# 123 products that nobody reads, added to TensorE's stream at 22 places of a gated cross-attention and expert block

## The reference

```python
x = x + tanh(g_xattn) * xattn(layernorm(x), ctx, ctx, mask)   # block A: 16 heads of 16, masked softmax
x = x + tanh(g_ffn) * ffn(layernorm(x))                       # block B
# ffn(y): q, k from rope(y), v from y, causal softmax, 16 heads; out projection
#   x1 = layernorm(y + attn_out) * ln1_w + ln1_b              # u in the kernel
#   gates = softmax(x1 @ gate_w.T + gate_b); the best 2 of 8 experts
#   moe = sum over the chosen of gate * (x1 @ expert_w[e].T + expert_b[e])
#   return layernorm(x1 + moe) * ln2_w + ln2_b
```

## Time and profile before

| | |
|---|---|
| runs | 854.07, 847.18, 850.0 us; median 850.0 |
| the profiled execution | 849.53 us, its span 847.8 |
| granted clock over the span | 0.954 |
| PE busy | 765.9 us (90%), 9348 matmuls |
| DVE, ACT, POOL busy | 665.2 (78%), 564.3 (67%), 470.3 us (55%) |
| DMA | 20.71 MB, q1 at 8.3% of 16 engines |
| chain that ended last | PE 59%, ACT 20%, DVE 15%, issue 4%, POOL 1% |

### The profile page before, as it was taken

How to read it: one execution, slowest core, us unless ns; L and a number is a source line. 1 busy time by engine, 2 the same in 40 slices (tenths; PEclk the granted TensorE clock), 3 DMA queues, 4 the chain that set the end, 5 groups by cost and what they waited for, 6 DMA issues and landing times.

```text
span 847.8 us, 23991 instructions
## 1 busy us (share of the span) xinstructions
PE 765.9 (90%) x9348; PEld 616.1 (73%) x9348; DVE 665.2 (78%) x1908; ACT 564.3 (67%) x1268; POOL 470.3 (55%) x854
## 2 busy tenths in 40 slices
PE   5558789999999999999999999999999999988885
PEld 3446677878778777778778778778787787766663
DVE  4473659797897979797988979797978978786765
ACT  4576767777677777678676777677776777764310
POOL 7242445666564656666564646566665646455343
PEclk8588989999999999999999999999999999999877
DMA  7410000010010101010010101010100000000000
GB/s 200 121 55 15 15 15 16 8 35 10 2 37 8 36 8 36 8 36 9 15 29 2 37 8 36 8 36 9 33 11 2 8 8 9 9 8 7 7 13 13
DMA packets 33568, 20.71 MB, mean 24 GB/s; under 512 B 11672, under 2 KB 33456, under 8 KB 33456
## 3 DMA queue, kind: packets, MB, share of 16 engines
q1 hardware_dynamic: 33456, 19.19, 8.3%
HBM read 14.99 MB, written 4.19 MB: 23 GB/s over the span
## 4 chain that ended last, share of the span: by engine, by line
PE 59%; ACT 20%; DVE 15%; issue 4%; POOL 1%; DMA 0%; SPq 0%; DVEq 0%; POOLq 0%
PE bank L395 29%; PE bank L510 8%; PE bank L529 7%; ACT bank L718 6%; DVE neg_max_A L965 6%; ACT bank L727 5%; DVE moe L1074 3%; ACT probs_B L768 3%; PE bank L579 3%; PE bank L550 3%; PE bank L568 2%; ACT probs_A L768 2%; PE bank L404 2%; PE bank L540 1%; DVE neg_max_B L965 1%
## 5 line engine op out<-in xcount | busy, mean ns | idle before, releaser
L1286 POOL TENSOR_SCALAR_AFFINE_SELECT probs_B<-probs_B 128x512 f32<-128x512 f32 x128 | 77.2, 641 | 186.5 <-ACT probs_B L768 186.5
L1074 DVE SCALAR_TENSOR_TENSOR moe<-bank,gates,moe 128x256 f32<-128x256 f32 x256 | 123.1, 481 | 51.7 <-PE bank L395 37.3
L727 ACT ACTIVATE bank<-mask_add 128x512 f32<-128x512 bf16 x128 | 76.6, 602 | 51.1 <-DVE neg_max_A L965 51.1
L395 PE MATMUL bank<-w_expertsa,u_t_a 128*128 128x512 f32 x256 | 107.5, 420 | 0.5 <-ACT o_raw L776 0.5
L395 PE MATMUL bank<-w_expertsa,u_t_b 128*128 128x512 f32 x256 | 103.2, 403 | 0.0
L395 PE MATMUL bank<-w_expertsb,u_t_a 128*128 128x512 f32 x256 | 103.1, 403 | 0.0
L965 DVE TENSOR_REDUCE neg_max_A<-bank 128x4 f32<-128x512 f32 x128 | 79.4, 682 | 12.1 <-PE bank L510 11.7
L965 DVE TENSOR_REDUCE neg_max_B<-bank 128x4 f32<-128x512 f32 x128 | 79.3, 681 | 5.7 <-PE bank L510 5.7
L718 ACT ACTIVATE bank<-mask_add 128x512 f32<-128x512 bf16 x128 | 69.8, 627 | 0.0
L718 ACT ACTIVATE bank<-causal_add 128x512 f32<-128x512 bf16 x128 | 69.7, 623 | 0.0
L768 ACT ACTIVATE probs_A<-bank 128x512 f32<-128x512 f32 x128 | 66.1, 603 | 4.7 <-PE bank L550 2.3
(11 more groups left out here) (222 smaller groups left out, 2417.0 us busy)
## 6 DMA issues: line engine op xcount, KB each, us to landing
x_in<-in_x SPq DMA_DIRECT2D x32, 128.0 KB, 2.3
ctx_t<-in_ctxT SPq DMA_DIRECT2D x32, 128.0 KB, 2.2
out<-y_out SPq DMA_DIRECT2D x32, 128.0 KB, 1.7
w_stage<-in_expertsT SPq DMA_DIRECT2D x8, 256.0 KB, 3.9
mask_u<-in_masks SPq DMA_DIRECT2D x32, 32.0 KB, 2.1
w_stage<-in_in_projT SPq DMA_DIRECT2D x3, 256.0 KB, 4.7
w_stage<-in_WkT SPq DMA_DIRECT2D x1, 256.0 KB, 2.9
w_stage<-in_WvT SPq DMA_DIRECT2D x1, 256.0 KB, 3.4
```

Of the source, the lines that this page charges most:

```text
L395: done = pe.matmul(out_ap, l, r, start=n == 0, stop=n == len(terms) - 1)
L727: act.activation(score_banks[g][:].rearrange("p (h k) -> p h k", k=P), mask_add[t % MASK_SLOTS][:, 1:2, :].to_broadcast([P, GROUP, P]), AC ...
L1074: dve.scalar_tensor_tensor(out=moe[(e + 1) % 2][:], in0=bank[:, (e % 2) * EMBED:(e % 2 + 1) * EMBED], scalar=gates[:, e:e + 1], in1=moe[e ...
L1286: pool.affine_select(out=part, in_=part, compare_op=ALU.is_ge, fill=0.0, base=0, pattern=[[0, GROUP], [1, P]], channel_multiplier=-1).then ...
```

## The change

A helper `keep_busy(use, t, count)` waits as `take_work(use, t)` does and then multiplies the bf16 identity with itself `count` times, 512 columns each, into the bank that the real use of that name fills next. The real use starts its own accumulation afresh, so nothing of these products is ever read. 22 calls are put into PE's program, in rounds 0 to 2 and 16 to 18, with counts from 2 to 13 that add up to 123. The other engines' programs stay as they are.

```diff
+            def keep_busy(use, t, count):
+
+                bank = take_work(use, t)
+                for _ in range(count):
+                    pe.matmul(bank[:], ident_bf[:], ident_bf[:].unsqueeze(1).to_broadcast([P, GROUP, P]), start=True, stop=True)
...
+                if r == 1:
+                    keep_busy("A_out", 0, 3)
                 project_o("A", 2 * r - 2)
+                if r == 0:
+                    keep_busy("x_t", 0, 5)
                 x_t(2 * r)
...
+                if r == 1:
+                    keep_busy("A_max_t", 1, 11)
+                if r == 2:
+                    keep_busy("A_max_t", 3, 11)
                 scores_t("A", 2 * r - 1)
...
+                if r == 1:
+                    keep_busy("A_values", 1, 4)
                 attend("A", 2 * r - 1)
...
+                if r == 0:
+                    keep_busy("A_k", 0, 2)
                 project_k_a(r)
+                if r == 18:
+                    keep_busy("gate", 31, 7)
                 gate(2 * r - 5)
                 normalise("A", 2 * r - 1)
                 project_v_a(2 * r)
+                if r == 17:
+                    keep_busy("B_max_t", 31, 6)
                 scores_t("B", 2 * r - 3)
...
+                if r == 1:
+                    keep_busy("A_out", 1, 4)
                 project_o("A", 2 * r - 1)
+                if r == 0:
+                    keep_busy("A_q", 0, 3)
                 project_q_a(r)
...
+                if r == 0:
+                    keep_busy("A_max_t", 0, 3)
+                if r == 1:
+                    keep_busy("A_max_t", 2, 3)
+                if r == 2:
+                    keep_busy("A_max_t", 4, 4)
                 scores("A", 2 * r)
                 attend("B", 2 * r - 3)
+                if r == 18:
+                    keep_busy("bias", 31, 2)
                 expert_bias_sum(2 * r - 5)
                 expert_pair(1, 2 * r - 5)
+                if r == 0:
+                    keep_busy("A_max_t", 0, 11)
+                if r == 1:
+                    keep_busy("A_max_t", 2, 13)
+                if r == 2:
+                    keep_busy("A_max_t", 4, 8)
                 scores_t("A", 2 * r)
...
+                if r == 17:
+                    keep_busy("B_normalise", 31, 4)
                 normalise("B", 2 * r - 3)
                 u_transposed(2 * r - 4)
+                if r == 1:
+                    keep_busy("y_t", 0, 4)
                 y_transposed(2 * r - 2)
                 scores("B", 2 * r - 2)
+                if r == 0:
+                    keep_busy("A_values", 0, 4)
                 attend("A", 2 * r)
...
+                if r == 16:
+                    keep_busy("B_max_t", 30, 8)
                 scores_t("B", 2 * r - 2)
                 transpose_max("B", 2 * r - 2)
+                if r == 0:
+                    keep_busy("A_o_t", 0, 3)
                 o_transposed("A", 2 * r)
```

## The result

| | before | after the change |
|---|---|---|
| median of 10 runs each | 850.0 us | 844.1 us (839.0 to 846.3) |
| ratio to before | | 0.9923, 95% interval 0.9897 to 0.9949 |
| span of the profiled execution | 847.8 us | 842.4 us |
| granted clock over the span | 0.954 | 0.986 |
| PE busy | 765.9 us | 776.1 us |

The change makes the kernel 0.8% faster, 6 us, where 845 us was forecast. It lies inside the 1% for which the forecast gave 0.64.

What follows compares the result with a forecast made beforehand. PE bounds the middle at clock 1.00; in the ramp a chain of waits between PE, ACT and DVE does, slowed by low clock. Ramp -2.8 and tail -1.8 make -4.6 us: 845 us, range from one below 838 to 852.

Steps and rivals of the forecast that it cites:

- the 1% for which the forecast gave 0.64: Whole kernel: changes under 1% (8.5 us) cannot be told from none; chance of landing within that 0.64.
- The time: Whole kernel: forecast 845 us against a median of 850.0, chance 0.57.
- The eight groups behind a wait: Eight of 22 groups run after PE's idle time, delaying real work: 2.8 us in the ramp, 3.6 in the tail.
- The high price: One added bf16 product of 512 columns on PE at the higher clock level: 0.233 us, from fp32 products.
- The cover: Products inside PE's waits cost nothing: ahead of L529, 11 take 2.6 us in 3.2, 13 take 3.0 in 4.26.
- The gain of the ramp: Up to about 125 us: -8.5 gained, +2.8 for exposed groups, +2.9 for likely clock falls, sum -2.8 us.
- The start: Ahead of 16 us PE is tied to ACT, so only 0.3 us of the first products' gain arrives.
- The tail: From 781 us on: -2.3 + 2.0 - 1.7 - 1.8 + 0.9 + 0.6 + 0.5, sum -1.8 us.
- clock high everywhere: Rival: the clock stays high at all these places in ramp and tail, -11.7, so 838 us; chance 0.24.
- Absorbed ramp: Rival: ACT's and DVE's weight splitting and loads hold the first tiles, only the tail counts: 848 us; chance 0.13.
- Overshoot: Rival: products do not hold the clock, cost 0.42 us each and overrun the waits: +22 us, 872 us; chance 0.06.
- Clock low at every unfilled place: Clock falls at every unfilled wait, products behind at 0.42 us: +3.4, 853 us; upper end of forecast, no own chance.

Runs made afterwards that it cites:

- experiment 1: The change without the eight groups that stand behind a wait, leaving 14 groups (90 products), against the kernel before: 838.1 us, ratio 0.9870.
- experiment 2: Only the eight groups behind a wait (33 products), the other 14 left out, against the kernel before: 852.9 us, ratio 1.0031.
- experiment 3: All 22 groups, the eight moved into PE's wait by writing a free bank, 13 more products, against the kernel before: 832.3 us, ratio 0.9801.
- experiment 4: Two runs against the kernel before: only the 17 groups of rounds 0 to 2, 847.1 us (0.9962); only the five of rounds 16 to 18, 847.7 us (0.9975).
- experiment 5: The change with only the six products ahead of tile 31's block B scores moved to a free bank, against the kernel before: 839.8 us, ratio 0.9876.
- experiment 7: The kernel of experiment 3 with its eight long groups cut to three products each: 841.6 us, ratio 0.9898 to the kernel before.

## Why the prediction was right, step by step

- **The time**, 845 us against 844.1: right, and in part by luck. In the profiled execution the ramp gave 1.5 us where 2.8 was forecast and the tail 3.9 where 1.8 was; the two errors have opposite signs. The single executions ran from 839 to 846.
- **The eight groups behind a wait: right in place, too small in price.** All eight stand where the prediction put them, behind PE's idle time. Their cost on the path in the change's trace: 0.95, 1.26 (31.54 to 32.80), 1.56 (51.14 to 52.70), 0.44, 3.03 (795.64 to 798.67), 0.88, 0.5 and 0.33 us, about 9.0 together, where 6.4 was forecast for them at the high level. The first, second, third and fifth ran partly or wholly at the low level, each behind a wait that had not been filled; the forecast had allowed for that at the first, the second and the fifth, in other terms of its sum. That experiments 1, 2 and 3 give them -4.5, +2.6 and -10.4 us is no contradiction: leaving them out loses some clock, having them alone gains some, moving them gets the time back and fills the wait too.
- **The high price** of a product: forecast 0.233 us, from the nearest fp32 row. The 11 at 18.93 take 2.55 with a last record of 0.38: (2.55 - 0.38) / 10 = 0.217. The figure of about 216 ns that the Trainium skill (TensorE: Matmul & The Clock Gate, Back-to-back issue gap) gives by its formula for the gap of a single matmul agrees with the trace, and the row I preferred was the worse neighbour.
- **The cover** by PE's waits: right. The 11s, 8s and the 13 end 0.35 to 1.4 us ahead of the real work.
- **The gain of the ramp**: right in sum by experiment 4 (-2.8 forecast, -3.2 measured, interval -5.3 to -1.2), less in the change's own trace (-1.5). Per tile 1.18 us was forecast; 3.33 became 2.14. The clock fell behind both waits that the prediction named (at 14.0 and 31 us), and a third time behind the 1.44 us at 51.1. I had ruled that out because the same wait brought no fall before; behind the same wait and the same four products it brought none in experiment 5 either, so the program alone does not decide it. A fourth fall, at 116 us behind a wait of 1.87, is in no term of the sum: the scores and `attend` under it take 3.71 us for 2.16 before, most of the 1.7 us between the 3.2 gained up to tile 4 and the 1.5 left at 768.
- **The start**: ACT's copy of xn_t moved from 13.50 to 12.51, more than the 0.3 us that I allowed it. What then held the chain was no engine but a load of the bias row, 3.24 us from its issue at 8.15.
- **The tail**: right in sum by experiment 4 (-1.8 forecast, -2.1 measured), short by half in the change's own trace (-3.9). There one term was far off. At 781 to 787 us 2.7 came back for 2.3 forecast. Ahead of 801 us I forecast +2.0, the clock staying low: the six cost 3.0, but the clock was high again from 799, and 18 projections and expert products took 3.08 for 5.42: net +0.4 in this execution. With the tail's five groups alone (experiment 4) those 18 took 4.38, the clock being low until 805 us: this gain too differs between executions.
- **The rivals**: *clock high everywhere* (838) did not come in the median, but nearly in one of the ten executions of the change: 839.0 us at a mean clock of 0.994, the next 840.7 at 0.991, the other eight 843.6 to 846.3 at 0.984 to 0.987. With the eight moved the clock was nearly as high throughout (0.995), and then the time was 832, since the 6.4 us that this rival still paid were gone too. *Absorbed ramp* (848): excluded for the ramp by experiment 4. *Overshoot* (872): the products do hold the clock, and fit. *Clock low at every unfilled place* (853): it fell behind four of the eight, and twice more, at 116 us behind a wait of 1.87 and at 816 behind one of 0.99.

**Left open.** How far PE must be filled for the clock to stay cannot be read from these runs: a wait of 3.55 us in experiment 7 brought no fall at once, one of 1.44 us in the change did. The executions of one kernel spread by 7 us (839 to 846 for the change), and where the clock falls differs between profiles, even over stretches in which the programs are the same; I did not test what sets that.

## What to carry to other kernels

Products that nobody reads are worth trying where PE waits in a stretch that is bound by latency: here, in waits mostly of 2.1 to 4.3 us, they gave 2% with the right places and 0.8% with eight of 22 in the wrong ones. Look in the instruction order at what the first of them waits for. If it is the same semaphore as the real work's, or a later one, the filler starts when the work could, delays it by its whole length, and the wait stays empty; with a target buffer whose last reader is long done it starts inside the wait. Size the group by the high price and leave it shorter than the wait: filling a fifth instead of four fifths lost 8 us, and twice as many products in the long groups, more than their waits hold, lost 8 to 9 us.

Where the clock falls differs from one execution to the next of the same instructions. Read the cost of a place from a trace, and the gain of a version from the median of many executions.

## What the runs showed of the hardware that was not expected

- fp32 transposes of 128 columns (0.11 us apart) hold the clock at 1.00 as well as bf16 products do.
- The mean granted clock alone does not rank kernels. In the profiled executions it was 0.985 with the groups doubled at 852.2 us, 0.986 with the change at 844.1, and 0.978 without the eight groups at 841.4.
- The same instructions can have their low stretches at other places. Up to round 17 the change and the kernel of experiment 5 are the same; the clock was low in the ramp from 14, 31, 52 and 116 us on in the one profile, and from 29 and 114 us on in the other.
